# Counting with sixteen accumulating matmuls instead of a VectorE sum, in the threshold search of an expert-choice layer

## The chip, the cores and the metric

The kernel runs on one core of one Trainium2 chip. The metric is the device time of one execution in microseconds (us), and a comparison goes by the median of several runs. Below, TensorE is PE in the rows, VectorE is DVE, ScalarE is ACT, GpSimd is POOL and SyncE is SP.

## The reference

The layer is a cross-attention with a residual, followed by a mixture of eight experts in which each expert chooses its tokens. The second half is where the change lies:

```
x = x + cross_attention(layernorm(x), ctx)          # x: 2 x 2048 x 512
xn = layernorm(x)
probs = softmax(xn @ gate_w.T)                      # 2 x 2048 x 8
g, m = top_k(probs transposed, k = 512)             # for each batch and expert: its 512 best tokens
h = gelu(xn[m] @ w1[e]) @ w2[e]                     # 512 x 512 -> 512 x 2048 -> 512 x 512
out = x + scatter_add(g * h at m)
```

So for each of 2 batches and 8 experts the 512 largest of 2048 probabilities are wanted.

## The kernel before

Tokens lie on partitions: a batch of 2048 tokens is 16 tiles of 128. The attention works through 16 blocks of two tiles (`step`), software-pipelined over five engines. In a step TensorE transposes the softmax of the block before (L969), multiplies the gate of an older block (L922, 16 matmuls of 8 columns), computes this block's scores (L940 to L942 with AH, AL: 48 matmuls of 308 columns, in four groups of 12), transposes the next block (L914, 8 matmuls) and multiplies the output of the block before (L940 to L942 with BH, BL: 30 matmuls of 512 columns with 8 transposes, L930, in their middle). Precision comes from splitting a number into a high and a low part, which is why matmuls come in threes. After the attention, 16 columns of work follow, one for each batch and expert; each goes through 16 hidden tiles f, an `up` of 12 and a `down` of 12 matmuls of 512 columns.

The top 512 are found without sorting. The kernel builds the 512th largest probability bit by bit, two bits in a round, in 15 rounds for each batch, for the eight experts at once. A round (`dve_round`) makes three candidate thresholds for each expert (`cand`, L471), compares all probabilities with them (`hit`, L474: 8 experts x 3 candidates x 16 tiles on each partition, bfloat16 zeros and ones), shifts the bits (L476), and sums `hit` over a partition's 16 tiles into `cnt` (L479). `pe_round` (L485) sums `cnt` over the 128 partitions by a matmul whose stationary operand is all ones, so the 24 counts stand on every partition of a PSUM bank. At the start of the next round `dve_narrow` reads them there (`kept`, L446), takes the best candidate that still has 512 hits (L449, L451), and the next candidates follow from it.

Where a round stands is written out by hand. Each engine runs its own instructions in their order. For batch 0 the rounds lie in the attention steps 10 to 15, three for a step, in slots:

- slot 2: VectorE does the round at the very end of step i, and TensorE does its matmul as the first thing of step i+1, ahead of the transposes L969 (rounds 0, 3, 6, 9, 12)
- slot 0: VectorE at the start of the step, TensorE behind the gate matmuls L922 and ahead of the scores
- slot 1: VectorE behind the split of the softmax (L843, L847), TensorE ahead of the last of the four groups of score matmuls

For batch 1 the 15 rounds lie in the first two expert columns, one for each hidden tile f, VectorE's part at the end of a tile and TensorE's behind the `up` matmuls (L1270 to L1272) of the next, ahead of a `down` (L1283 to L1285). A similar block of 16 small accumulating matmuls exists already: `pe_lookup` (L582), where a one-hot matrix picks the chosen tokens' numbers, 20 columns in each. `cnt` is used once more per batch, in `dve_masks` (L494) and `pe_before` (L501), for 8 columns.

On GpSimd, the last work of a step is the scaling of the softmax (L707, once for each tile) and the addition of the bias to the residual (L696).

Of the kernel before, what the change touches and what calls it, by code (L numbers as in the profile page):

```python
# [7 lines left out]
BF16 = mybir.dt.bfloat16  # L8
U32 = mybir.dt.uint32
ACT = mybir.ActivationFunctionType  # L10
AX = mybir.AxisListType

P = 128
# [3 lines left out]
E, F = 8, 2048  # L17
# [10 lines left out]
NT = S // P  # L28
# [4 lines left out]
CAND = 3  # L33
ROUNDS = 15
# [3 lines left out]
def xattn_expert_choice(nc, x, ctx, wq, wk, wv, wo, bo, gate_w, w1, w2, out):  # L38
# [6 lines left out]
    top = ExitStack()  # L45
    with top:
        def sb(scope, name, shape, dt=F32):
            return scope.enter_context(nc.sbuf_tensor(name, shape, dt))

        def sem(name):  # L50
            return top.enter_context(nc.semaphore(name))
# [3 lines left out]
        ones_bf = sb(top, "ones_bf", [P, P], BF16)  # L55
# [39 lines left out]
        kept = sb(top, "kept", [P, E, CAND])  # L95
        best = sb(top, "best", [P, E])
        hit = sb(top, "hit", [P, E, CAND, NT], BF16)
        cnt = sb(top, "cnt", [P, E * CAND], BF16)
        above = sb(top, "above", [P, E, NT], BF16)
        tied = sb(top, "tied", [P, E, NT], BF16)  # L100
        chosen = sb(top, "chosen", [P, E, NT], BF16)
# [279 lines left out]
        def tile_scores(t):  # L381
# [8 lines left out]

        (s_init, s_bits, s_cand, s_hit, s_cnt, s_tot, s_kept, s_best, s_thr, s_link, s_mask, s_before, s_placed,
         s_vals, h_hot, h_used, h_found, h_fsum, h_idx) = (sem(n) for n in (
             "s_init s_bits s_cand s_hit s_cnt s_tot s_kept s_best s_thr s_link s_mask s_before s_placed "
             "s_vals h_hot h_used h_found h_fsum h_idx").split())
        SLOTS = 3
        GATED = NBLK // B + 2
# [13 lines left out]
        def choice(bank):  # L412


            inside, sums = ps[:, bank, 128:128 + E * NT], ps[:, bank, 256:256 + E * NT]
            return inside, sums, ps[:, bank, 384:384 + E * CAND], ps[:, bank, 416:416 + NV * CT]
# [3 lines left out]
        def round_bank(b, k):  # L420

            return BANK[1] if b == 1 else 0 if k % SLOTS == 0 else 3
# [3 lines left out]
        def link(ins):  # L426

            chained[0] += 1
            ins.then_inc(s_link, 1)
            nc.vector.wait_ge(s_link, chained[0])  # L430

        def u32(t):
            return t[:].bitcast(U32)
# [4 lines left out]
        def each_cand(t):  # L438
            return t.unsqueeze(2).broadcast_to([P, E, CAND])

        def dve_narrow(dve, b, k):

            n = b * ROUNDS + k + 1
            counts = choice(round_bank(b, k))[2].rearrange("p (e m) -> p e m", m=CAND)
            dve.wait_ge(s_tot, n)
            nc.vector.scalar_tensor_tensor(out=kept[:], in0=counts, scalar=float(CAP), in1=cand[:],  # L446
                                           op0=ALU.is_ge, op1=ALU.mult).then_inc(s_kept, 1)
            dve.wait_ge(s_kept, n)
            nc.vector.tensor_reduce(best[:], kept[:], AX.X, ALU.max).then_inc(s_best, 1)  # L449
            dve.wait_ge(s_best, n)  # L450
            nc.vector.tensor_tensor(thr[:], thr[:], best[:], ALU.max).then_inc(s_thr, 1)  # L451

        def dve_round(dve, b, k):


            n = b * ROUNDS + k + 1
            if k == 0:
                dve.wait_ge(v_gate, (b + 1) * (NBLK // B))
                if b == 0:
                    nc.vector.memset(chain[:], 1.0)  # L460
                    link(nc.vector.memset(hit[:, 0, 0, 0:1], 0.0))
                    nc.vector.memset(chain[:, :, 0:1], 0.0)
                for m in range(CAND):
                    nc.vector.memset(bits[:, :, m:m + 1], 2.0 ** (32 * m - 95))
                nc.vector.memset(thr[:], 0.0).then_inc(s_init, 1)
                dve.wait_ge(s_init, b + 1)
            else:
                dve_narrow(dve, b, k - 1)
                dve.wait_ge(s_thr, n - 1)
                dve.wait_ge(s_bits, n - 1)  # L470
            nc.vector.tensor_tensor(u32(cand), each_cand(u32(thr)), u32(bits), ALU.bitwise_or).then_inc(s_cand, 1)  # L471
            dve.wait_ge(s_cand, n)
            shape = [P, E, CAND, NT]
            nc.vector.tensor_tensor(hit[:], probs[:, b].unsqueeze(2).broadcast_to(shape),  # L474
                                    cand[:].unsqueeze(3).broadcast_to(shape), ALU.is_ge).then_inc(s_hit, 1)
            nc.vector.tensor_scalar(u32(bits), u32(bits), 2, None, ALU.logical_shift_right).then_inc(s_bits, 1)  # L476
            dve.wait_ge(s_hit, n)
            with nc.allow_low_precision(reason="counts up to 16 are exact in bfloat16"):
                nc.vector.tensor_reduce(cnt[:], hit[:].rearrange("p e m t -> p (e m) t"), AX.X,  # L479
                                        ALU.add).then_inc(s_cnt, 1)  # L480

        def pe_round(pe, b, k):

            pe.wait_ge(s_cnt, b * ROUNDS + k + 1)
            nc.tensor.matmul(choice(round_bank(b, k))[2], ones_bf[:], cnt[:], start=True, stop=True).then_inc(s_tot, 1)  # L485

        def dve_masks(dve, b):

# [329 lines left out]
        def dve_attention(dve):  # L818
# [16 lines left out]
            def step(i, u, half, has):  # L835
                if round_at(i, 0) is not None:
                    dve_round(dve, 0, round_at(i, 0))
# [12 lines left out]
                if round_at(i, 1) is not None:  # L850
                    dve_round(dve, 0, round_at(i, 1))
# [43 lines left out]
                if round_at(i, 2) is not None:  # L895
                    dve_round(dve, 0, round_at(i, 2))
# [37 lines left out]
        def pe_attention(pe):  # L934
# [17 lines left out]
            def step(i, u, half, has):  # L952
                if round_at(i - 1, 2) is not None:
                    pe_round(pe, 0, round_at(i - 1, 2))
# [19 lines left out]
                if round_at(i, 0) is not None:  # L974
                    pe_round(pe, 0, round_at(i, 0))
                if at(i, 0):
                    pe.wait_ge(e_lo, NA)
                if has(i):
                    pe.wait_ge(v_xTl, i + 1)
                    if isinstance(i, int):  # L980
                        batch = i // (NBLK // B)
                        base = [batch * KD * HJ + dk * HJ for dk in range(KD)]
                    else:
                        base0 = pe.snap(i // (NBLK // B) * (KD * HJ))
                        base = [base0 + dk * HJ for dk in range(KD)]
                    fh, fl = (m[:].rearrange("p b k n -> p (b k n)") for m in (AH, AL))
                    for t in range(TPB):
                        for part in range(2):
                            if has(i - 1) and (t, part) == (0, 1):
                                pe.wait_ge(v_tails, i)  # L990
                            if has(i - 3) and (t, part) == (1, 1):
                                pe.wait_ge(v_gsub, i - 2)
                            if round_at(i, 1) is not None and (t, part) == (1, 1):
                                pe_round(pe, 0, round_at(i, 1))
                            last = three(ps[:, 2 * t + part, 0:HALF],
                                         [(xTh[:, t, dk * P:(dk + 1) * P], xTl[:, t, dk * P:(dk + 1) * P],
                                           fh[:, bass.ds(base[dk] + part * HALF, HALF)],
                                           fl[:, bass.ds(base[dk] + part * HALF, HALF)])
                                          for dk in range(KD)])
                        last.then_inc(p_s, 1)  # L1000
# [380 lines left out]
```

## Time and profile before

| | us |
|---|---|
| median of 3 runs | 1841.84 |
| lowest and highest of them | 1840.74, 1842.87 |
| span of the profiled execution | 1840.1 |
| busy in it: TensorE (matmul) | 1789.4 |
| busy: VectorE | 972.9 |
| busy: ScalarE | 674.0 |
| busy: GpSimd | 307.6 |

The span runs from the first to the last instruction of one execution; the median of the runs lies 1.7 us above it, and the profiled execution has no other time of its own in the profile. Busy shares are means over stages with different limits: attention lies in the first 390 us, the experts behind it. A row of a timeline gives the start, the duration, the engine, the line and what it writes and reads; in square brackets stands how long the engine had been idle and who ended that. Matmuls overlap, so that the cost of one in a row of equal ones is the distance of the starts and not its duration.

### The profile page before, as it was taken

The page shows a single profiled execution, that of the slowest core. Times are in us where ns is not written, and L with a number is a line of the kernel's source. Part 1 is how long each engine was busy: PE and PEld are TensorE (multiplying, and loading weights), DVE is VectorE, ACT ScalarE, POOL GpSimd, SP SyncE. Part 2 cuts the span into 40 slices and gives each one's busy share as a digit, 9 for nine tenths or more (in the row PEclk, how much of TensorE's full clock was granted, in tenths as well). Part 3 has the DMA queues.
Part 4 walks back from the last instruction along what each step waited for, and adds up shares of the span by engine and source line. Part 5 has one row for each costly group of instructions (what it writes and reads, how often), then busy time and mean ns, then how long its engine had stood idle before and what let it go on. Part 6 is the DMA issues. An engine that isn't in the chain of part 4 may idle for free.

```text
span 1840.1 us, 25378 instructions
## 1 busy us (share of the span) xinstructions
PE 1789.4 (97%) x8786; PEld 1500.9 (82%) x8786; DVE 972.9 (53%) x1910; ACT 674.0 (37%) x1546; POOL 307.6 (17%) x353
## 2 busy tenths in 40 slices
PE   7999999889999999999999999999999999999996
PEld 6799988767888888888888888888888888888885
DVE  5555577767766454545454545454545454545442
ACT  3556544453333333333333333333323333333321
POOL 2334333220202020202020202020202020111101
PEclk9999988889999999999999999999999999999998
DMA  3242324233434252535252425252525252525221
GB/s 132 71 136 92 136 87 154 73 115 111 120 109 128 102 138 106 142 108 143 93 137 91 137 91 137 91 137 91 137 91 137 91 147 87 163 71 170 72 89 23
DMA packets 101699, 206.39 MB, mean 112 GB/s; under 512 B 5235, under 2 KB 5389, under 8 KB 101653
## 3 DMA queue, kind: packets, MB, share of 16 engines
q1 hardware_dynamic: 87317, 172.23, 26.4%
q0 software_dynamic: 14336, 33.56, 10.0%
q8 instruction: 27, 0.44, 0.1%
q14 instruction: 19, 0.16, 0.0%
HBM read 172.22 MB, written 33.55 MB: 112 GB/s over the span
## 4 chain that ended last, share of the span: by engine, by line
PE 94%; DVE 2%; ACT 2%; DMA 1%; issue 0%; POOL 0%; SPq 0%; POOLq 0%; DVEq 0%; ACTq 0%
PE ps L1283 13%; PE ps L1270 13%; PE ps L1272 13%; PE ps L1271 13%; PE ps L1285 13%; PE ps L1284 13%; PE ps L940 4%; PE ps L941 3%; PE ps L942 3%; PE ps L922 2%; PE ps L1254 2%; PE ps L969 1%; ACT PR L738 1%; PE ps L914 1%; PE ps L282 1%; DVE cand L471 1%
## 5 line engine op out<-in xcount | busy, mean ns | idle before, releaser
L1147 ACT ACTIVATE hf<-ps 128x512 f32<-128x512 f32 x256 | 153.1, 598 | 855.7 <-PE ps L1272 855.7
L1200 DVE CAST hh<-hf 128x512 fp32r<-128x512 f32 x256 | 110.2, 430 | 600.4 <-ACT hf L1147 600.4
L1270 PE MATMUL ps<-eTh,w1h 128*128 (+1 forms) x1024 | 404.2, 395 | 1.5 <-issue 1.5
L1283 PE MATMUL ps<-w2h,hh 128*128 128x512 f32 x1024 | 401.4, 392 | 0.0
L1272 PE MATMUL ps<-eTh,w1l 128*128 (+1 forms) x1024 | 399.0, 390 | 0.0
L1285 PE MATMUL ps<-w2h,hl 128*128 128x512 f32 x1024 | 398.9, 390 | 0.0
L1284 PE MATMUL ps<-w2l,hh 128*128 128x512 f32 x1024 | 398.7, 389 | 0.0
L1271 PE MATMUL ps<-eTl,w1h 128*128 (+1 forms) x1024 | 398.6, 389 | 0.0
L1104 POOL DMA_INDIRECT out_dram<-Y,sidx x64 | 105.0, 1641 | 1082.0 <-DVE Y L1236 1000.2
L1272 PEld LDWEIGHTS ps<-eTh,w1l 128*128 128x128 f32 x1024 | 192.2, 188 | 40.5
L1285 PEld LDWEIGHTS ps<-w2h,hl 128*128 128x128 f32 x1024 | 192.3, 188 | 40.3
L1270 PEld LDWEIGHTS ps<-eTh,w1h 128*128 128x128 f32 x1024 | 192.4, 188 | 39.4 <-issue 1.7
L1283 PEld LDWEIGHTS ps<-w2h,hh 128*128 128x128 f32 x1024 | 192.4, 188 | 39.0
L1284 PEld LDWEIGHTS ps<-w2l,hh 128*128 128x128 f32 x1024 | 192.3, 188 | 38.9
L1271 PEld LDWEIGHTS ps<-eTl,w1h 128*128 128x128 f32 x1024 | 192.5, 188 | 38.1
L1181 DVE TENSOR_TENSOR w1l<-w_raw,w1h 128x512 fp32r<-128x512 f32 x256 | 175.2, 684 | 29.6 <-ACT w1h L1125 29.5
L1202 DVE TENSOR_TENSOR hl<-hf,hh 128x512 fp32r<-128x512 f32 x256 | 177.4, 693 | 8.8
L1184 DVE TENSOR_TENSOR w2l<-w_raw,w2h 128x512 fp32r<-128x512 f32 x256 | 175.2, 684 | 0.0
L1125 ACT ACTIVATE w1h<-w_raw 128x512 fp32r<-128x512 f32 x256 | 160.2, 626 | 0.0
L1129 ACT ACTIVATE w2h<-w_raw 128x512 fp32r<-128x512 f32 x256 | 160.1, 626 | 0.0
L738 ACT ACTIVATE PR<-ps,nmax 128x77 f32<-128x77 f32 x256 | 78.7, 333 | 52.2 <-DVE nmax L832 52.2
L940 PE MATMUL ps<-AH,xTh 128*128 128x308 f32 (+1 forms) x256 | 84.2, 329 | 1.6 <-DVE AL L296 1.6
(156 smaller groups left out, 1798.7 us busy)
## 6 DMA issues: line engine op xcount, KB each, us to landing
w_raw<-in_L_ffn_w_dram SPq DMA_DIRECT2D x128, 1024.0 KB, 7.2
XB<-in_x_dram SPq DMA_DIRECT2D x16, 512.0 KB, 4.0
XR<-in_x_dram SPq DMA_DIRECT2D x16, 512.0 KB, 3.6
out_dram<-X SPq DMA_DIRECT2D x16, 512.0 KB, 4.7
xn_rows<-XN SPq DMA_DIRECT2D x16, 512.0 KB, 5.4
w_raw<-in_L_xattn_Wq_dram SPq DMA_DIRECT2D x1, 1024.0 KB, 10.0
w_raw<-in_L_xattn_Wo_dram SPq DMA_DIRECT2D x1, 1024.0 KB, 13.2
XB<-xn_rows,gidx POOLq DMA_INDIRECT x64
```

Source lines behind the costliest of these rows:

```text
L940: nc.tensor.matmul(psum, wh, mh, start=(k == 0), stop=False, **kw)
L1125: nc.scalar.activation(w1h[:, f % SLOTS1], w1_raw[:, g % 2, :, j * P:(j + 1) * P], ACT.Copy).then_inc(f_w1h, 1)
L1129: nc.scalar.activation(w2h[:, f % SLOTS2], w2_raw[:, g % 2, j, :], ACT.Copy).then_inc(f_w2h, 1)
L1181: nc.vector.tensor_tensor(w1l[:, f % SLOTS1], w1_raw[:, g % 2, :, j * P:(j + 1) * P], w1h[:, f % SLOTS1].bitcast(F32), ALU.subtract).then_ ...
L1184: nc.vector.tensor_tensor(w2l[:, f % SLOTS2], w2_raw[:, g % 2, j, :], w2h[:, f % SLOTS2].bitcast(F32), ALU.subtract).then_inc(f_w2l, 1)
L1202: nc.vector.tensor_tensor(hl[:, f % 4], hf[:, f % 2, :], hh[:, f % 4].bitcast(F32), ALU.subtract).then_inc(f_h, 1)
L1270: nc.tensor.matmul(ps[:, 4 + f % 2, :], wh, flat_eTh[:, chunk], start=(k == 0), stop=False)
L1271: nc.tensor.matmul(ps[:, 4 + f % 2, :], wh, flat_eTl[:, chunk], start=False, stop=False)
L1272: last = nc.tensor.matmul(ps[:, 4 + f % 2, :], wl, flat_eTh[:, chunk], start=False, stop=(k == KD - 1))
L1283: nc.tensor.matmul(ps[:, c, :], th, wh, start=(f == 0), stop=False)
L1284: nc.tensor.matmul(ps[:, c, :], th, wl, start=False, stop=False)
L1285: last = nc.tensor.matmul(ps[:, c, :], tl, wh, start=False, stop=(f == KF - 1))
```

## The change

The sum on VectorE (L479) goes, with its semaphore `s_cnt`. TensorE now waits for `hit` itself, and counts over the tiles too: 16 matmuls with the all-ones stationary operand, one for each tile t, accumulate in the same PSUM bank. Each reads 24 columns of `hit`; since t is the innermost index of `hit`, two neighbouring columns lie 16 elements (32 bytes) apart, where the 24 columns of `cnt` lay side by side. `cnt` shrinks to the 8 columns that its other use needs.

```diff
-        cnt = sb(top, "cnt", [P, E * CAND], BF16)
+        cnt = sb(top, "cnt", [P, E], BF16)
...
             nc.vector.tensor_scalar(u32(bits), u32(bits), 2, None, ALU.logical_shift_right).then_inc(s_bits, 1)
-            dve.wait_ge(s_hit, n)
-            with nc.allow_low_precision(reason="counts up to 16 are exact in bfloat16"):
-                nc.vector.tensor_reduce(cnt[:], hit[:].rearrange("p e m t -> p (e m) t"), AX.X,
-                                        ALU.add).then_inc(s_cnt, 1)

         def pe_round(pe, b, k):

-            pe.wait_ge(s_cnt, b * ROUNDS + k + 1)
-            nc.tensor.matmul(choice(round_bank(b, k))[2], ones_bf[:], cnt[:], start=True, stop=True).then_inc(s_tot, 1)
+            pe.wait_ge(s_hit, b * ROUNDS + k + 1)
+            counts = choice(round_bank(b, k))[2].rearrange("p (e m) -> p e m", m=CAND)
+            for t in range(NT):
+                last = nc.tensor.matmul(counts, ones_bf[:], hit[:, :, :, t], start=(t == 0), stop=(t == NT - 1))
+            last.then_inc(s_tot, 1)
```

On TensorE, a slot 2 round followed by a slot 0 round in the attention, before the change:

```order
L941 MATMUL ps<-BL,pTh 128x512
L942 MATMUL ps<-BH,pTl 128x512
L485 MATMUL ps<-cnt,ones_bf 128x24
L969 MATMUL ps<-ident,PR 128x128 x4
L969 MATMUL ps<-ident,PR 104x128
L969 MATMUL ps<-ident,PR 128x128 x4
L969 MATMUL ps<-ident,PR 104x128
L922 MATMUL ps<-gwT,xn2T 128x8 x8
L485 MATMUL ps<-cnt,ones_bf 128x24
L940 MATMUL ps<-AH,xTh 128x308
```

The same place with the change (its line numbers are smaller by one or two from here on):

```order
L940 MATMUL ps<-BL,pTh 128x512
L941 MATMUL ps<-BH,pTl 128x512
L483 MATMUL ps<-hit,ones_bf 128x24 x16
L968 MATMUL ps<-ident,PR 128x128 x4
L968 MATMUL ps<-ident,PR 104x128
L968 MATMUL ps<-ident,PR 128x128 x4
L968 MATMUL ps<-ident,PR 104x128
L921 MATMUL ps<-gwT,xn2T 128x8 x8
L483 MATMUL ps<-hit,ones_bf 128x24 x16
L939 MATMUL ps<-AH,xTh 128x308
```

Nothing changes places; each round's single matmul is now a block of 16. On VectorE, a slot 0 round and what follows it, before:

```order
L471 TENSOR_TENSOR cand<-thr,bits 128x24
L474 TENSOR_TENSOR hit<-probs,cand 128x384
L476 TENSOR_SCALAR bits<-bits 128x24
L479 TENSOR_REDUCE cnt<-hit 128x24
L843 TENSOR_TENSOR pTl<-ps,pTh 104x2x128
```

And with the change:

```order
L471 TENSOR_TENSOR cand<-thr,bits 128x24
L474 TENSOR_TENSOR hit<-probs,cand 128x384
L476 TENSOR_SCALAR bits<-bits 128x24
L842 TENSOR_TENSOR pTl<-ps,pTh 104x2x128
```

The sum has gone from the end of the round, and `hit` is now the last of it that TensorE waits for.

## Rows read from the trace of the kernel before

**Rows 1.** The page's parts 1, 2 and 4, whole span.

```profile
PE 1789.4 (97%) x8786; PEld 1500.9 (82%) x8786; DVE 972.9 (53%) x1910; ACT 674.0 (37%) x1546; POOL 307.6 (17%) x353
...
PEclk9999988889999999999999999999999999999998
...
PE 94%; DVE 2%; ACT 2%; DMA 1%; issue 0%; POOL 0%; SPq 0%; POOLq 0%; DVEq 0%; ACTq 0%
```

**Rows 2.** Waits, whole span: engine and line, waited for whom, us, times, longest.

```profile
PE ps L485 <- DVE cnt L479: 10.8, 5, 2.2
```

**Rows 3.** Chain that ended last, 250 to 266 us: start, us, what.

```profile
249.93 0.26 PE ps L940
...
250.33 0.14 PE ps L942
...
254.42 0.89 PE ps L914 x8
...
255.33 0.89 ACT xTh L731
...
256.26 1.52 ACT XN L724 x2
257.78 2.45 ACT PR L738 x16
...
260.75 1.04 DVE thr L451
...
261.81 2.33 DVE cand L471
...
264.16 0.56 DVE hit L474
...
264.81 0.51 DVE cnt L479
...
265.37 0.19 PE ps L485
```

**Rows 4.** Timeline of GpSimd, 257 to 273 us.

```profile
260.54 1.22 POOL L707 TENSOR_TENSOR PR<-PR,srec 128x616 f32<-128x616 f32 x1 [1.52 <-DVE srec L823]
261.71 2.38 POOL L696 TENSOR_TENSOR XR<-XR,bo_rows 128x1024 f32<-128x1024 f32 x1
```

**Rows 5.** Timeline of TensorE at slot 2 rounds and at the end of attention.

```profile
241.20 0.19 PE L485 MATMUL ps<-cnt,ones_bf 128*128 128x24 bf16 x1 [2.09 <-DVE cnt L479]
...
242.42 2.67 PE L922 MATMUL ps<-gwT,xn2T 128*128 128x8 f32 x16
...
337.93 0.19 PE L485 MATMUL ps<-cnt,ones_bf 128*128 128x24 bf16 x1 [2.15 <-DVE cnt L479]
...
360.67 0.23 PE L503 MATMUL ps<-chosen,before_bf 128*128 128x128 bf16 x1 [1.35 <-DVE chosen L524]
```

**Rows 6.** Timeline of TensorE in a step without rounds.

```profile
221.61 1.85 PE L922 MATMUL ps<-gwT,xn2T 128*128 128x8 f32 x16
```

**Rows 7.** Timeline of TensorE in the experts: a block of lookups, a round.

```profile
407.46 0.56 PE L582 MATMUL ps<-vals,hot 128*128 128x20 bf16 x16
407.88 0.47 PE L1283 MATMUL ps<-w2h,hh 128*128 128x512 f32 x1
...
413.44 0.19 PE L485 MATMUL ps<-cnt,ones_bf 128*128 128x24 bf16 x1
413.48 0.47 PE L1283 MATMUL ps<-w2h,hh 128*128 128x512 f32 x1
```

**Rows 8.** Stretches: us, busy of PE, PEld, DVE, ACT, POOL; granted clock; DMA.

```profile
44.90:48.60 3.70, 1.76 (x4) 0.87 (x5) 1.49 (x3) 1.65 (x7) 2.10 (x2) 1.00 0.02 4
...
243.30:250.00 6.70, 6.70 (x30) 6.70 (x30) 4.92 (x13) 0.83 (x2) 0.00 (x0) 0.50 0.07 21
...
362.80:372.90 10.10, 7.90 (x24) 6.47 (x23) 6.77 (x14) 0.59 (x1) 0.00 (x0) 0.50 0.14 54
400.00:515.00 115.00, 115.00 (x557) 92.54 (x556) 85.63 (x220) 40.95 (x72) 16.65 (x16) 1.00 0.42 130
```

More of the change, by code:

```diff
@@ L387, in xattn_expert_choice @@
         gate_sc7 = ps[:, 7, 0:TPB * E].rearrange("p (t e) -> p t e", e=E)
-        (s_init, s_bits, s_cand, s_hit, s_cnt, s_tot, s_kept, s_best, s_thr, s_link, s_mask, s_before, s_placed,
+        (s_init, s_bits, s_cand, s_hit, s_tot, s_kept, s_best, s_thr, s_link, s_mask, s_before, s_placed,
          s_vals, h_hot, h_used, h_found, h_fsum, h_idx) = (sem(n) for n in (
-             "s_init s_bits s_cand s_hit s_cnt s_tot s_kept s_best s_thr s_link s_mask s_before s_placed "
+             "s_init s_bits s_cand s_hit s_tot s_kept s_best s_thr s_link s_mask s_before s_placed "
              "s_vals h_hot h_used h_found h_fsum h_idx").split())
```

## The prediction

> **What bounds the kernel now.** I read the page first: busy shares, clock line, chain [rows 1]. TensorE is busy for 97% of the span and the chain is 94% TensorE, so a matmul more costs its time nearly everywhere, and work taken off VectorE (53% busy) gains nothing unless TensorE waits for just that. The list of waits says where it does: five times for `cnt`, 10.8 us in all [rows 2]. The clock digits are 8 instead of 9 in four of the slices, the ones that hold the attention rounds. So there are two stages with different answers.
>
> The first is attention with rounds. The timeline has the five waits at the slot 2 rounds, from 241.20 to 337.93 us, 24.18 us apart ((337.93 - 241.20) / 4) [rows 5]. The chain shows a full step [rows 3]: the last score matmuls, the transposes L914, ScalarE (0.89, 1.52 and 2.45 us), then VectorE with `thr` 1.04, `cand` 2.33, `hit` 0.56 and `cnt` 0.51 us, and at 265.37 TensorE again. All that TensorE does from a slot 2 round to L914 is on this chain, as is the sum. `thr` and `cand` work on 24 numbers or fewer for each partition and yet take 1 and 2.3 us; they end with GpSimd's operations that started at 260.54 and 261.71 and ran 1.22 and 2.38 us [rows 4]. Whatever comes of the sum, these stay ahead of `hit`.
>
> Behind each of these waits the granted clock falls: 0.50 of full speed, that is 1.2 in place of 2.4 GHz, from 243.3 to 250.0 us [rows 8]. A score matmul goes every 0.26 us there and every 0.14 us behind it [rows 3]; the 16 gate matmuls take 2.67 us against 1.85 in a step without rounds [rows 5, 6]. Five slot 2 rounds, five such falls; I saw nothing of the kind in steps without rounds.
>
> The second stage is the experts. From 400 to 515 us, with all 15 rounds of batch 1, TensorE is busy for 115.00 of 115 us at full clock [rows 8]. No wait for `cnt` is there to be won.
>
> **The change part by part.**
>
> The price of a block. No row shows 24 strided columns against all ones. The nearest one is the lookup block: 16 bfloat16 matmuls of 20 columns; the block starts at 407.46 and the next matmul at 407.88, so 0.42 us, 0.026 for each. A single round takes 413.48 - 413.44 = 0.04 us [rows 7]. So a block costs 0.42 - 0.04 = 0.38 us more at full clock, and I take twice that, 0.77 us, at half clock. It can't be below nothing: 16 matmuls stand where one stood, and nothing hides them on an engine that has no gap. From above, the dearest narrow matmuls are the gates, 16 in 1.85 us [rows 6]: 1.8 us more for each round. I take 0.38, since type, shape and count agree with the lookups best.
>
> Experts. 15 rounds x 0.38 = +5.7 us. VectorE's 15 sums there are worth nothing, their engine is not waited for.
>
> Attention, clock as before. Slot 2: the sum leaves the chain; TensorE can start some 0.06 us after `hit` ends (264.16 + 0.56 = 264.72), so at 264.78 in place of 265.37, -0.59 us; its block +0.38. Slot 0 runs behind the gates, at half clock: +0.77. Slot 1 runs ahead of the last scores at full clock: +0.38. All three blocks lie between a slot 2 round and L914, on the chain. One step: -0.59 + 0.38 + 0.77 + 0.38 = +0.94 us, five steps +4.7 us. The ten sums of slots 0 and 1 gain nothing, VectorE has idle time later in the step.
>
> What is queued behind the new wait. `kept` (L446) waits for the 16th matmul instead of the only one, up to 0.8 us later. Behind it in VectorE's queue stand the split of the softmax, the gate's subtraction and the residual; TensorE wants them some microseconds later. Cost taken as 0; if that cover is gone, at most 0.8 us a step. No DMA and nothing on SP's or GpSimd's queues moves.
>
> The clock. This is the largest term, and it is not fixed by the sum above. TensorE's idle time ahead of a slot 2 round shrinks from 2.1 to some 1.5 us, and behind it comes a block of real matmuls. Does the clock still fall? For it: after an idle time of only 1.35 us at 360.67, followed by the same transposes and gates, it stood at 0.50 from 362.8 to 372.9 [rows 5, 8]. Against it: from 44.9 to 48.6 TensorE was busy for 1.76 of 3.70 us, with 512-column matmuls, and kept 1.00 [rows 8]. The new rounds lie between these. Each fall that goes gives back, in the scores, from the gates' end (242.42 + 2.67 = 245.1) to 250.0 us, (4.9 / 0.26 =) 19 matmuls x (0.26 - 0.14) = 2.3 us, in the gates 2.67 - 1.85 = 0.8 us, and 0.4 us of the slot 0 block: 3.5 us, less some 0.1 us since the first gates run ahead of the fall: 3.4 us. If all five stay, the total is +5.7 + 4.7 = +10.4; if all go, 10.4 - 17 = -6.6. I take two or three of five: 10.4 - 2.5 x 3.4 = +1.9 us.
>
> TensorE: Matmul & The Clock Gate, § Part 1 of the Trainium skill, says that this clock follows how busy TensorE has been and that the chip's watch on it runs freely beside the kernel, not from its start. The trace agrees as to the two levels (1.00 and 0.50). By this rule the number of falls may differ from one run to the next. No row here shows several executions.
>
> **Sum.** Against the profiled execution's span, 1840.1 + 1.9 = 1842.0 us; the median of the runs lies 1.7 us above that span, so about 1844 us.
>
> **The rivals.**
>
> A. All falls of the clock stay. For it: the 1.35 us case. Against: 0.6 us less idle, and a block of matmuls in the place of one. +10.4: about 1852 us.
>
> B. All, or all but one, go. Attention then gains more than the experts lose: -6.6 to -3.2 us, 1835 to 1839. For it: the idle time is the only thing that these steps have and the earlier steps lack. Against: slot 2 block, transposes, gates and slot 0 block now are one long run of narrow matmuls, and the gates did nothing to keep the clock up at 360.67.
>
> C. Strided columns are slow, and the rounds are plainly dearer. The place is the moving operand of the 480 new matmuls, whose columns are 32 bytes apart. A score matmul takes 0.14 us for 308 four-byte columns lying side by side, 0.46 ns for each [rows 3]. If a column that has no neighbour costs four of these, 24 cost 44 ns, more than the 26 ns of a lookup, and a block takes 0.70 us: +0.66 at full, +1.3 at half clock. Experts 15 x 0.66 = 9.9; attention 5 x (-0.59 + 0.66 + 1.3 + 0.66) = 10.2; total +20 with all falls kept, about 1862 us, or 1858 with one gone. It decides from the point at which a column costs more than 26 / 24 = 1.1 ns; below that it hides behind what a small matmul takes anyway. Against it: nothing in the trace, which has no strided moving operand.
>
> Beside C stands a rule of the Trainium skill that speaks against this change: SBUF — State Buffer, § Door 1: The DMA port swizzle, holds that reads go at full rate while they stay in one 16-byte line, with at least two hits in each, and pay at every crossing to a new line. By it each of the 24 columns is a crossing. The rule gives no price, and no row here can show it; by it the sum is C's.
>
> **How the numbers follow.** Within 0.2% (3.7 us) a measurement of this kernel can't tell a change from none. Forecast (two or three falls gone, cheap columns), 0.37: 1840.3 to 1847, of it 0.06 faster, 0.24 same, 0.07 slower. A, 0.21: 0.02 same, 0.19 slower. B, 0.16: 0.14 faster, 0.02 same. C, 0.26: 0.02 same (falls gone as well), 0.24 slower. Together faster 0.20, same 0.30, slower 0.50. The range takes in nearly all of B at the bottom and C with one fall gone at the top: 1834 to 1860.
>
> **What would show it.** The 16 matmuls of a round: first start to next matmul's start 0.42 us if columns are cheap, 0.7 if C holds. The wait of slot 2 rounds is for `hit`, near 1.5 us, five times. VectorE's busy time falls by 30 x 0.51 = 15 us or a little more. In the experts TensorE stays full and the round stretch is 5.7 us longer. Stretches at 0.50: five like 243 to 250 under A, none under B; each one more or less is 3.4 us. The forecast is wrong if the clock shows the same five falls, if a block takes over 0.5 us, or if TensorE waits elsewhere for what `kept` now delays.

## The result and the profile after

The changed kernel takes 1862.77 us (median of 4 runs, 1862.34 to 1863.71) against 1842.09 us: a ratio of 1.0113, with a 95% interval of 1.0101 to 1.0126. It is slower by 20.7 us, where 1844 us was forecast with a range up to 1860. The spans of the two profiled executions differ by 20.9 us (1861.0 and 1840.1).

The page after, the lines that answer to [rows 1]:

```profile
PE 1814.3 (97%) x9236; PEld 1524.8 (82%) x9236; DVE 959.0 (52%) x1880; ACT 673.9 (36%) x1546; POOL 307.0 (16%) x353
...
PEclk9999988889999999999999999999999999999998
...
PE 94%; DVE 2%; ACT 2%; issue 1%; DMA 1%; POOL 0%; SPq 0%; POOLq 0%; DVEq 0%; ACTq 0%
```

TensorE has 450 instructions more, which is 30 x 15, and the same share of the span; VectorE has 30 fewer and lost 14 us that nobody waited for. The waits after, as in [rows 2]:

```profile
DVE kept L446 <- PE ps L483: 10.3, 9, 1.4
...
PE ps L483 <- DVE hit L474: 7.8, 5, 1.6
```

TensorE's five waits shrank from 10.8 to 7.8 us, 0.6 us each, as worked out. The new wait of `kept` for the sixteenth matmul shows up on VectorE. So that part went as forecast, and the loss must lie in the blocks and the clock. TensorE's timeline after, at the slot 2 and slot 0 rounds, as in [rows 5], and in the experts, as in [rows 7]:

```profile
240.58 0.90 PE L483 MATMUL ps<-hit,ones_bf 128*128 128x24 bf16 x16 [1.52 <-DVE hit L474]
241.30 1.29 PE L968 MATMUL ps<-ident,PR 128*128 128x128 f32 x10
...
245.18 0.91 PE L483 MATMUL ps<-hit,ones_bf 128*128 128x24 bf16 x16
245.91 0.60 PE L939 MATMUL ps<-AH,xTh 128*128 128x308 f32 x1
...
265.86 0.90 PE L483 MATMUL ps<-hit,ones_bf 128*128 128x24 bf16 x16 [1.58 <-DVE hit L474]
...
292.75 0.91 PE L483 MATMUL ps<-hit,ones_bf 128*128 128x24 bf16 x16 [1.57 <-DVE hit L474]
...
530.66 0.91 PE L483 MATMUL ps<-hit,ones_bf 128*128 128x24 bf16 x16
531.39 0.49 PE L1282 MATMUL ps<-w2h,hh 128*128 128x512 f32 x1
```

From one block's start to the next matmul's are 0.73 us (531.39 - 530.66), not 0.42: nearly 0.046 us for each matmul. The last block in the experts starts 20.2 us later than the last round did before (at 510.51 there). And the block at 245.18, at half clock, takes 0.73 us as well (245.91 - 245.18). The steps, from slot 2 round to slot 2 round, last 25.28 us (265.86 - 240.58) and then 26.89 (292.75 - 265.86), where they lasted 24.18. The stretches say why two lengths, and that the experts have no gap still; columns as in [rows 8]:

```profile
243.10:249.70 6.60, 6.60 (x42) 6.60 (x42) 4.36 (x11) 1.04 (x2) 0.00 (x0) 0.50 0.09 34
267.00:277.00 10.00, 10.00 (x58) 9.99 (x58) 5.97 (x18) 1.52 (x3) 0.00 (x0) 0.50 0.18 68
...
294.30:304.30 10.00, 10.00 (x58) 10.00 (x57) 5.25 (x14) 1.52 (x3) 0.00 (x0) 0.50 0.11 23
400.00:532.00 132.00, 132.00 (x822) 108.38 (x821) 82.90 (x213) 47.92 (x82) 15.78 (x16) 1.00 0.36 111
```

The clock still falls in every one of the five steps with rounds. In two of them it stays at 0.50 for about 7 us, as before, and in three for about 10 us (the rows show two of these).

The account: 15 blocks in the experts x (0.73 - 0.04) = 10.3 us. The rest came before the experts: the first slot 2 round starts 0.6 us earlier, the first `pe_before` 10.1 us later (365.57 against 355.46). Together 20.4 of 20.9 us.

The 10.1 us have two parts. A step with a fall as long as before is 1.1 us longer (25.28 - 24.18), which makes 5.5 us for five. The three longer falls make up the other 4.6 us.

### The profile page after: what moved, and what is told of

Read it like the earlier page. It is cut to its first block, busy times and chain, and to the rows that moved or that the text cites. A ratio compares the mean times of both kernels' runs of the same rounds, so it can differ in the third digit from the quotient of the medians.

```text
span 1861.0 us, 26248 instructions
## 1 busy us (share of the span) xinstructions
PE 1814.3 (97%) x9236; PEld 1524.8 (82%) x9236; DVE 959.0 (52%) x1880; ACT 673.9 (36%) x1546; POOL 307.0 (16%) x353
## 4 chain that ended last, share of the span: by engine, by line
PE 94%; DVE 2%; ACT 2%; issue 1%; DMA 1%; POOL 0%; SPq 0%; POOLq 0%; DVEq 0%; ACTq 0%
PE ps L1282 13%; PE ps L1269 13%; PE ps L1271 13%; PE ps L1283 12%; PE ps L1270 12%; PE ps L1284 12%; PE ps L939 4%; PE ps L940 3%; PE ps L941 3%; PE ps L921 2%; PE ps L1253 2%; PE ps L483 1%; PE ps L968 1%; ACT PR L737 1%; PE ps L913 1%
```

## The experiments

**What a column costs by its distance.** The kernel before, with 16 probing matmuls behind each count:

```diff
+        PROBES = ((1, 24), (4, 24), (2, 24), (8, 24), (16, 24), (8, 46), (16, 4), (8, 24), (16, 8), (16, 12), (1, 24),
+                  (16, 16), (4, 64), (1, 64), (16, 20))
...
+            step, n = PROBES[k]
+            flat = hit[:].rearrange("p e m t -> p (e m t)")
+            for t in range(NT):
+                last = nc.tensor.matmul(ps[:, round_bank(b, k), 440:440 + n], ones_bf[:],
+                                        flat[:, bass.ds(t % 4, n, step=step)], start=(t == 0), stop=(t == NT - 1))
```

`PROBES` gives the step in elements of 2 bytes and the number of columns for each of the 15 rounds.

> The kernel before, counting as it did (sum on VectorE, one matmul), with 16 further matmuls behind each count that read hit at a given step and width and write unused PSUM columns: steps of 1, 2, 4, 8 and 16 elements with 24 columns, step 16 with 4, 8, 12, 16 and 20 columns, step 8 with 46, steps 1 and 4 with 64. Only the cost of a block is read from it. Theory (a column in a 16-byte piece of its own is what costs): 24 columns at step 1, 2 and 4 go at 0.026 to 0.03 us each, at steps 8 and 16 at 0.045; at step 16 the cost grows by 1.9 ns for each column above some 14 columns, and 4, 8 and 12 columns cost 0.026; a block at half clock and step 8 or 16 costs the same 0.72 us as at full clock. Rival (it is the count of 16 accumulating matmuls with the same stationary operand, whatever they read): all 24-column blocks cost 0.72 us at every step.

TensorE's timeline, each block with the matmul behind it. The first two blocks are out of the attention, at half clock: 24 columns at step 16, and 64 side by side. The others are out of the experts, at full clock. In order they are 24 columns at step 4, 8 and 16; 46 at step 8; 12 and 16 at step 16; 64 at step 4; 64 side by side; 20 at step 16.

```profile
271.26 0.90 PE L492 MATMUL ps<-hit,ones_bf 128*128 128x24 bf16 x16
271.99 0.61 PE L949 MATMUL ps<-AH,xTh 128*128 128x308 f32 x1
...
353.15 1.01 PE L492 MATMUL ps<-hit,ones_bf 128*128 128x64 bf16 x16
353.97 0.61 PE L949 MATMUL ps<-AH,xTh 128*128 128x308 f32 x1
...
431.66 0.56 PE L492 MATMUL ps<-hit,ones_bf 128*128 128x24 bf16 x16
432.07 0.47 PE L1292 MATMUL ps<-w2h,hh 128*128 128x512 f32 x1
...
443.62 0.90 PE L492 MATMUL ps<-hit,ones_bf 128*128 128x24 bf16 x16
444.35 0.48 PE L1292 MATMUL ps<-w2h,hh 128*128 128x512 f32 x1
...
449.95 0.90 PE L492 MATMUL ps<-hit,ones_bf 128*128 128x24 bf16 x16
450.67 0.48 PE L1292 MATMUL ps<-w2h,hh 128*128 128x512 f32 x1
...
456.73 1.51 PE L492 MATMUL ps<-hit,ones_bf 128*128 128x46 bf16 x16
458.03 0.47 PE L1292 MATMUL ps<-w2h,hh 128*128 128x512 f32 x1
...
482.92 0.58 PE L492 MATMUL ps<-hit,ones_bf 128*128 128x12 bf16 x16
483.35 0.47 PE L1292 MATMUL ps<-w2h,hh 128*128 128x512 f32 x1
...
495.39 0.67 PE L492 MATMUL ps<-hit,ones_bf 128*128 128x16 bf16 x16
495.90 0.48 PE L1292 MATMUL ps<-w2h,hh 128*128 128x512 f32 x1
...
506.92 1.12 PE L492 MATMUL ps<-hit,ones_bf 128*128 128x64 bf16 x16
507.84 0.48 PE L1279 MATMUL ps<-eTh,w1h 128*128 128x512 f32 x1
...
524.89 0.64 PE L492 MATMUL ps<-hit,ones_bf 128*128 128x64 bf16 x16
525.36 0.47 PE L1292 MATMUL ps<-w2h,hh 128*128 128x512 f32 x1
...
530.97 0.78 PE L492 MATMUL ps<-hit,ones_bf 128*128 128x20 bf16 x16
531.58 0.48 PE L1292 MATMUL ps<-w2h,hh 128*128 128x512 f32 x1
```

| columns, step (bytes) | block, us | one matmul, ns |
|---|---|---|
| 24, 8 bytes | 0.41 | 26 |
| 24, 16 bytes | 0.73 | 45 |
| 24, 32 bytes | 0.72 | 45 |
| 24, 32 bytes, at half clock | 0.73 | 45 |
| 12 / 16 / 20, 32 bytes | 0.43 / 0.51 / 0.61 | 27 / 32 / 38 |
| 46, 16 bytes | 1.30 | 81 |
| 64, 8 bytes | 0.92 | 57 |
| 64, side by side | 0.47 | 30 |
| 64, side by side, at half clock | 0.82 | 51 |

These rows fit one rule: a matmul takes at least 26 ns, and at least 1.8 to 2 ns for each 16-byte piece that it touches. 24 and 20 pieces take 45 and 38 ns, 46 take 81 ns; 64 columns at 8 bytes are 32 pieces and take 57 ns, 1.8 each; 24 at 8 bytes are 12 pieces, hidden under the 26. Columns side by side touch so few pieces that something else bounds them. The matmul count alone is excluded: at 8 bytes the same 16 accumulating matmuls with the same weights cost 0.41 us. The price of a piece is the same at both clocks. That of adjacent columns is not: 64 of them take 30 ns at full clock and 51 at half.

SBUF — State Buffer, § Door 1: The DMA port swizzle of the Trainium skill has this line of 16 bytes and a penalty for every crossing to a new one; the trace agrees, and adds the number. The same section of the Trainium skill wants two hits in a line for full rate. Here the trace does not agree: 64 columns at a step of 8 bytes hit each line twice and take 57 ns, where 64 side by side take 30.

**The change with adjacent columns, VectorE writing with a stride.**

```diff
-        hit = sb(top, "hit", [P, E, CAND, NT], BF16)
+        hit = sb(top, "hit", [P, NT, E, CAND], BF16)
...
-            nc.vector.tensor_tensor(hit[:], probs[:, b].unsqueeze(2).broadcast_to(shape),
+            nc.vector.tensor_tensor(hit[:].rearrange("p t e m -> p e m t"), probs[:, b].unsqueeze(2).broadcast_to(shape),
...
-                last = nc.tensor.matmul(counts, ones_bf[:], hit[:, :, :, t], start=(t == 0), stop=(t == NT - 1))
+                last = nc.tensor.matmul(counts, ones_bf[:], hit[:, t, :, :], start=(t == 0), stop=(t == NT - 1))
```

> The changed kernel with hit stored tile by tile, so that the 24 columns of each matmul lie side by side; VectorE's comparison writes with a stride instead. Theory (strided columns are the dear part): blocks fall from 0.72 to 0.42 us, 15 x 0.30 = 4.5 us less in the experts and about 5 x 0.9 = 4.5 us less in attention, and one to three low-clock stretches fewer: 1862.8 - 9 - (0 to 10), so 1843 to 1854 us. Rival (the number of matmuls is dear): unchanged at 1862 us. If VectorE's comparison becomes slower by writing with a stride, each slot 2 wait grows by that much, at most 5 x 0.5 us.

1860.92 us, ratio 1.0112 (1.0097 to 1.0128): no better than the change. Both theories missed, because the edit changed two things. The groups of this kernel:

```profile
L474 DVE TENSOR_TENSOR hit<-probs,cand 128x384 bf16<-128x384 f32 x30 | 60.5, 2018 | 1.1
...
L483 PE MATMUL ps<-hit,ones_bf 128*128 128x24 bf16 x480 | 17.1, 176 | 14.7 <-DVE hit L474 14.7
```

The blocks are cheap, but the comparison takes 2.0 us in the mean where it took 0.63: VectorE writes 384 bfloat16 elements 48 bytes apart in 1.92 to 1.97 us instead of 0.56. I had allowed it 0.5 us more. It stands right ahead of the waits, which come to 14.7 us against 7.8 in the changed kernel and 10.8 before. That takes back most of the 9 us that 30 cheaper blocks are worth.

**The same in the five slot 2 rounds only**, with that strided write in all 30 rounds. A function `direct` says for which rounds the 16 matmuls stand; the others sum on VectorE and do one:

```diff
+            return b == 0 and k % SLOTS == 0
```

> The change made only in the five rounds for which TensorE waits (slot 2 of batch 0), with hit stored tile by tile; the other 25 rounds sum on VectorE as before. Theory: each slot 2 round gains 0.59 and pays 0.38 us, -1 us in all, and if the shorter idle time keeps the clock up in some steps 3 us more for each: 1830 to 1842 us. Rival (the fall of the clock doesn't depend on half a microsecond of idle time): 1841 to 1842 us with five falls as before. If VectorE's strided write or its strided sum is slower, up to 3 us more.

1854.85 us, 1.0076 (1.0062 to 1.0090), a miss for the same reason: the five waits come to 15.2 us. VectorE's sum, reading with a stride, also went from 0.55 to 0.83 us, and in the experts TensorE was idle for 1.9 of the 120 us from 400 on, where it had been busy throughout. These two kernels say nothing against adjacent columns, only against paying for them on VectorE.

**Adjacent on both sides.** VectorE's comparison now runs tile by tile too, and reads `probs` with a stride:

```diff
-            nc.vector.tensor_tensor(hit[:], probs[:, b].unsqueeze(2).broadcast_to(shape),
-                                    cand[:].unsqueeze(3).broadcast_to(shape), ALU.is_ge).then_inc(s_hit, 1)
+            nc.vector.tensor_tensor(hit[:], probs[:, b].rearrange("p e t -> p t e").unsqueeze(3).broadcast_to(shape),
+                                    cand[:].unsqueeze(1).broadcast_to(shape), ALU.is_ge).then_inc(s_hit, 1)
```

> The changed kernel with hit stored tile by tile and VectorE's comparison also running tile by tile, so that neither the write nor the matmuls' reads are strided (it reads probs with a stride instead). Theory (two prices of stride, 0.30 us for a block on TensorE and 1.4 us for a strided write on VectorE, hid each other in the earlier run): comparison near 0.56 us, blocks 0.42 us; experts +5.7, attention 5 x (-0.59 + 3 x 0.38) = +2.8 us, so +8.5 over the kernel before and 1849 us, with up to one fall of the clock (3 us) more or less. Rival (strided reading on VectorE costs as much as strided writing): comparison near 1.9 us and 1860 us again.

1846.10 us, 1.0021 (1.0005 to 1.0037). The groups:

```profile
L474 DVE TENSOR_TENSOR hit<-probs,cand 128x384 bf16<-128x384 f32 x30 | 18.9, 628 | 1.1
...
L483 PE MATMUL ps<-hit,ones_bf 128*128 128x24 bf16 x480 | 16.9, 174 | 7.8 <-DVE hit L474 7.8
```

The comparison is as fast as in the changed kernel, so reading `probs` in this order costs VectorE nothing. Only the columns' distance on TensorE differs from the changed kernel, and 17 of its 20.7 us are gone. That is more than the blocks hold, 30 x 0.31 = 9.3 us. The rest goes with the clock (below), whose falls here come in three of the five steps. The runs of this kernel spread from 1839 to 1851 us. The forecast of 1844 us had been for a kernel like this one.

**The two halves.** The change in batch 1's rounds alone, and in batch 0's alone (both strided, as in the diff):

```diff
+            return b == 1
```

That is `direct` in the first; the second has `b == 0`.

> The change made in batch 1's rounds alone (experts); batch 0's rounds in the attention are as before. Theory: 15 blocks at 0.72 instead of 0.04 us on an engine without gaps, 15 x 0.68 = +10.2 us over the kernel before, 1852.3 us, and the clock pattern of attention as before. Rival (the attention part carries nearly all, through the clock): +3 us or less.

> The change made in batch 0's rounds alone (attention), with strided columns; the experts' rounds are as before. Theory: what is left of the whole, 20.7 - 9.8 = +10.9 us: 5 x (-0.59 + 3 x 0.68) = +7.3 us of work and 3 to 4 us by a longer time at the lower clock, 1852 us. Rival (the two halves are not additive): more than 2 us away from that.

Experts only: 1850.40 us, 1.0055 (1.0041 to 1.0069), 9.8 us over the kernel before beside it. Attention only: 1848.89 us, 1.0038 (1.0018 to 1.0058), 6.8 us, with runs from 1842 to 1855. The first fits its 10.3 us. The second is 4 us below what the sum wanted, and more than 2 us was named as the sign that the halves don't add up. Its trace says where at least part of the 4 us went: in the first of the five steps the clock did not fall, and that step took 22.48 us (261.76 - 239.28) instead of 25.28. The attention code is that of the changed kernel. So the strided blocks alone do not fix the number of falls, and additivity is not shown closely.

**What the sum is worth when nothing is paid for it.** The sum is left out, and one matmul counts the first tile only.

```diff
-            for t in range(NT):
-                last = nc.tensor.matmul(counts, ones_bf[:], hit[:, :, :, t], start=(t == 0), stop=(t == NT - 1))
+            last = nc.tensor.matmul(counts, ones_bf[:], hit[:, :, :, 0], start=True, stop=True)
```

> The sum on VectorE is left out in all 30 rounds, and one matmul counts the hits of the first tile only, so the thresholds are not the reference's. It prices what taking the sum away is worth by itself. Theory: 5 x 0.59 = -3 us in attention, nothing in the experts, 1838 us, with at most one fall of the clock less (another -3). Rival (the sum matters in all rounds, or the falls of the clock go once the idle time is 1.5 us): 1825 to 1832 us.

1828.89 us, 0.9923 (0.9904 to 0.9943): 13.2 us faster, not 3. The rival's range had it. The waits give only 2.8 us of it (10.8 to 8.0). The rest goes with the clock. The stretch 200 to 400 us (us, busy as in [rows 8], clock) of, in turn, the kernel before, the changed one, the one adjacent on both sides and this one:

```profile
200.00:400.00 200.00, 178.07 (x1017) 160.68 (x1016) 139.62 (x349) 93.89 (x312) 59.29 (x84) 0.87 0.32 108
```

```profile
200.00:400.00 200.00, 181.06 (x1186) 165.11 (x1185) 125.42 (x318) 86.37 (x302) 59.45 (x84) 0.85 0.31 106
```

```profile
200.00:400.00 200.00, 181.03 (x1263) 163.43 (x1263) 135.26 (x337) 96.72 (x315) 59.59 (x84) 0.90 0.33 111
```

```profile
200.00:400.00 200.00, 181.41 (x1093) 162.51 (x1092) 141.96 (x364) 102.40 (x323) 60.59 (x86) 0.92 0.35 119
```

With two levels, 1.00 and 0.50, the time at the lower one is 2 x (1 - mean) x 200 us: 52, 60, 40 and 32 us. So this kernel, with half a microsecond less idle time in five places, was 20 us less at the low clock, and the changed one 8 us more. These are single executions, and the falls differ from one to the next. All runs together bear the order out: the mean granted clock of the span was 0.981 to 0.984 in the kernel before, 0.980 to 0.982 in the changed one, 0.982 to 0.990 with adjacent columns on both sides and 0.988 to 0.991 here. How much of the 8 us comes of the strided blocks is open: the kernel with the change in the experts only has the attention of the kernel before, and in its trace two of the five falls were 10 us long as well.

**A version from it.** 16 matmuls only where TensorE waits, in slot 2, out of a second tile written tile by tile; the other 25 rounds as before.

```diff
+        hit2 = sb(top, "hit2", [P, NT, E, CAND], BF16)
...
+            return b == 0 and k % SLOTS == 0
...
+                    last = nc.tensor.matmul(counts, ones_bf[:], hit2[:, t, :, :], start=(t == 0), stop=(t == NT - 1))
```

> The sixteen matmuls only in the five slot 2 rounds of batch 0, from a second tile written tile by tile; the other 25 rounds keep the first tile, the sum and one matmul. Theory: the wait shrinks by 0.59 us and the block costs 0.38, -1 us in all, 1839 to 1842 us; if the shorter idle time keeps the clock up, 3 us less for each step. Rival (the falls follow from idle time and narrow matmuls alike, so shifting time from one to the other leaves them): five falls as before and the same time within its interval.

> The two-tile kernel once more, on the same chip as the one beside it. Theory: its gain of some 0.4% over the kernel before is its own: ratio 0.994 to 0.998. Rival (it was the lot of where the clock's changes fell in those runs): ratio 0.998 to 1.001.

1834.49 us, 0.9957 (0.9941 to 0.9972), and again 1834.44 us, 0.9965 (0.9953 to 0.9977): faster than the kernel before by 7.6 and 6.3 us, and so than the changed one. A block of it, from the first profiled execution:

```profile
239.31 0.56 PE L500 MATMUL ps<-hit,ones_bf 128*128 128x24 bf16 x16 [1.49 <-DVE hit L481]
239.73 1.29 PE L988 MATMUL ps<-ident,PR 128*128 128x128 f32 x10
240.85 1.85 PE L941 MATMUL ps<-gwT,xn2T 128*128 128x8 f32 x16
242.56 0.17 PE L504 MATMUL ps<-cnt,ones_bf 128*128 128x24 bf16 x1
```

A block takes 0.42 us; the gates of this step take 1.85 us, so the clock did not fall here. The arithmetic of work alone gives -1 us; the rest goes with the clock. But how often it falls is not set by the code: in this execution it fell in four of the five steps, in the profiled one of the second set in two. There the slot 2 round at 262.80 us had waited 2.16 us, as long as in the kernel before, and the clock stayed at 1.00.

**Four wide matmuls instead.** As the last, but with 4 matmuls of 96 adjacent columns in place of its 16, and the remaining sum of four on VectorE after them:

```diff
+                for a in range(NT // 4):
+                    last = nc.tensor.matmul(ps[:, round_bank(b, k), 384:384 + n], ones_bf[:],
+                                            flat[:, a * n:(a + 1) * n], start=(a == 0), stop=(a == NT // 4 - 1))
...
+                link(nc.vector.tensor_reduce(four[:], parts, AX.X, ALU.add))
```

> As the two-tile kernel (sixteen matmuls in the five slot 2 rounds only), but with 4 matmuls of 96 adjacent columns in place of 16 of 24; what is left of the sum, 4 numbers to each count, VectorE adds up after the matmuls, where TensorE is busy with transposes and gates. Theory: a block of 4 takes about 0.17 us instead of 0.42 (0.04 us for each 96 columns), the sum after it costs nothing, since slot 0's block comes some 3 us later: 5 x 0.25 = 1.3 us less than the two-tile kernel, 1833 us, with up to one fall of the clock (3 us) more or less. Rival (VectorE's added sum delays slot 0's comparison past TensorE's gates): as much as the two-tile kernel or more.

1832.21 us, 0.9956 (0.9942 to 0.9969). Its block:

```profile
262.81 0.34 PE L506 MATMUL ps<-hit,ones_bf 128*128 128x96 bf16 x4 [2.25 <-DVE hit L486]
262.99 1.27 PE L995 MATMUL ps<-ident,PR 128*128 128x128 f32 x10
264.10 1.85 PE L948 MATMUL ps<-gwT,xn2T 128*128 128x8 f32 x16
```

0.18 us for the block, as expected. The added sum was free in four of five places; once, at 266.52 us, TensorE waited 0.57 us for the slot 0 count behind it. Its median is the lowest of all kernels that compute the whole, but the interval overlaps with the two-tile kernel's beside it (0.9953 to 0.9977); which is faster of the two is open.

## Why the prediction was wrong

- **The price of a block** is the step that failed first. I took the lookup's 0.42 us "since type, shape and count agree with the lookups best". They agree in all but the distance of the columns, and that was the part that counts: 0.73 us. The added price is 0.69 us for each round instead of 0.38. In the experts that makes 10.3 instead of 5.7 us. With adjacent columns and nothing else of TensorE's changed, 17 of the 20.7 us go. Rival C, with its guess that a lone column costs four adjacent ones, said 44 ns and the trace says 45. It was given 0.26; the rule beside it, which names the mechanism, deserved more than a lookup with adjacent columns.
- **Twice as dear at half clock** (0.77 us added) was wrong for both kinds. A strided block takes 0.73 us at either clock, and an adjacent one 0.43 us instead of 0.42 (a block of the kernel adjacent on both sides). So slot 0 cost 0.69 us more, and not 1.3 as in C. This is also why a step grew by 1.1 us only, where -0.57 + 3 x 0.69 gives 1.5: the fall ends near 250 us in both kernels, but the scores begin at 245.91 instead of 244.98, so fewer of them lie in it, and the slot 0 block in their place costs no more than at full clock.
- **The wait shrinks by 0.59 us**: right (2.09 to 1.52 us; 10.8 to 7.8 in all). Nothing in the experts came of the sum: right.
- **Two or three of five falls go** is the second step that failed, and the larger term: -8.5 us were put in the sum, and +4.6 us came, since in the profiled execution all five stayed and three of them lasted longer. Of the 18.5 us between the +1.9 of the sum and the 20.4 accounted for, 13.1 lie here, 4.6 in the experts' blocks and 0.8 in the attention's work. The two failures are not separate. With cheap blocks falls do go: in the kernel adjacent on both sides two of five are gone, and in the two-tile kernel's traces one and three. But one was gone as well in the trace of the strided kernel changed in attention only, so their number was in part chance.
- **C's 1862 us** came out so closely by luck. Its mechanism was right, but its slot 0 price was too high by some 3 us and it kept the falls at their length; the longer falls, 26.89 against 25.28 us a step, made up for that.
- **What is queued behind the new wait costs nothing**: VectorE's `kept` waited 10.3 us instead of 3.0, and TensorE's list of waits has no new entry. Right.
- The forecast's own size for a cheap block was sound: with adjacent columns it takes 0.42 us, and the kernel adjacent on both sides has 1846.1 us.

What decides whether the clock falls in a given step, and for how long, is not settled. Two things go with more low time in the stretches above. One is idle time ahead of the transposes: with one matmul in a round, five waits of 10.8 us in all had 52 us at the low clock and 8.0 us had 32. The other is the block behind the wait: with waits near 8 us throughout, blocks of 0.04, 0.42 and 0.73 us had 32, 40 and 60. The mean clocks of all runs have the same order.

Chance has a part too. The prediction took the stretch from 44.9 to 48.6 us [rows 8] as a sign that such a gap leaves the clock up. That code is the same in every kernel here, with a wait of 2.20 us before L282, and in eight of the twelve traces the clock did fall there. Two rows show it, from the kernel before and the one with four wide matmuls:

```profile
48.00:50.00 2.00, 2.00 (x6) 0.76 (x4) 0.51 (x1) 0.60 (x1) 0.00 (x0) 1.00 0.04 8
```

```profile
48.00:50.00 2.00, 2.00 (x4) 0.94 (x3) 0.34 (x1) 0.60 (x1) 0.00 (x0) 0.50 0.00 0
```

## What to carry to other kernels

Before a matmul reads its moving operand with a stride, count the 16-byte pieces that it touches and not its columns, above all if it is narrow; the layout has to be had from the writer, and here VectorE paid for writing 2-byte elements apart, and not for reading 4-byte ones apart. An accumulating block of matmuls is worth putting in place of a VectorE step only where TensorE waits for that step. And where a stage sits at the edge of a fall of the clock, a half microsecond of idle time can count several times (five of them, 13.2 us here), so one trace is not enough to count falls by.

## What the runs showed of the hardware

- A strided bfloat16 moving operand costs 1.8 to 2 ns for each 16 bytes touched, where that comes to more than the 26 ns of a small matmul. With 24 such columns it is 45 ns whether TensorE runs at 2.4 or at 1.2 GHz. A matmul of 24 adjacent columns is hardly slower at 1.2 GHz either (a block 0.43 against 0.42 us), but one of 64 is (51 against 30 ns).
- Two columns in each 16 bytes are not enough for the full rate: 64 of them took 57 ns, 64 side by side 30.
- VectorE wrote 384 bfloat16 elements 48 bytes apart in 1.92 to 1.97 us against 0.56 side by side; reading float32 64 bytes apart, each number for three results, at adjacent writes cost nothing (0.56 us).
- The granted clock's falls differ between executions of one code, and a kernel's time scatters with them. The kernel adjacent on both sides ran from 1839 to 1851 us: its three fastest runs had a mean granted clock of 0.990, its three slowest 0.982 to 0.984. The one changed in attention only ran from 1842 to 1855, while the kernel before stayed within 1838 to 1846. TensorE: Matmul & The Clock Gate, § Part 1 of the Trainium skill has the watch on TensorE running freely beside the kernel; the scatter, and the clock that falls at 48 us in one execution and not in another, agree with it.
